# A four-stage transformer kernel on one core: x fetched per batch, a small constant tile, and late weight copies on ScalarE

## The chip, the cores and the metric

The kernel runs on one core of one Trainium2 chip. The metric is the device time of one execution in microseconds (us): the median of three runs of the kernel before. Lower is better.

## What is computed

The reference takes x of shape 32 x 256 x 128 (32 batches of 256 tokens, width 128) and sends it through four stages, each with a residual sum and a layer norm behind it:

```python
x = L0_attn_x
x = _layernorm(x + _L0_attn_ref(x, L0_attn_w_qkv, L0_attn_w_out, L0_attn_b_out), axis=-1)
x = _layernorm(x + _L0_ffn_ref(x, L0_ffn_W_fc, L0_ffn_ln_w, L0_ffn_ln_b, L0_ffn_W_proj), axis=-1)
x = _layernorm(x + _L1_attn_ref(x, L1_attn_ln_g, L1_attn_ln_b, L1_attn_W_kv, L1_attn_W_x, L1_attn_W_xa, L1_attn_W_out), axis=-1)
x = _layernorm(x + _L1_ffn_ref(x, L1_ffn_w_gate, L1_ffn_w_up, L1_ffn_w_down), axis=-1)
return x
```

The first attention has 16 heads of width 8 with rotary embedding. The first feed-forward rounds its weights to -1, 0 and 1 against their mean magnitude. The second attention mixes its heads by a 16 x 16 matrix. The second feed-forward scales integer weights by 1/127 and gates with silu.

## The kernel before

The program runs five sequences, one for each engine, that are written out by hand in `program`. Each phase (`early` and `late` of the preparation, `attn0`, `ffn0`, `attn1`, `ffn1`) gives each engine a step for one batch, and the engines meet only in semaphores. Software pipelining is explicit: in step i an engine works on batches i-2 to i+4. The first attention has 32 steps and some before and behind them; the middle ones run in a loop of two steps per turn, one for even and one for odd batches. Nothing reorders the instructions: each engine takes them as they are written.

**Preparation.** `early` loads the attention's weights (`raw_qkv`, `raw_out`), turns them on TensorE and copies them out of PSUM on VectorE (`w0_qk`, `w0_v`, `w0_out`); the copies set `attn_taken`, for which TensorE waits before it turns the first x. GpSimd fills `ident`, `zeros` and both `stack` buffers. SyncE waits for `stacks_set`, then writes the free slots of the DRAM scratch (`score_parts`) out of `stack`, and only then issues the first two loads of x (`x_in`, step -4 and -3). `late` prepares all other weights. On SyncE it issues the loads of `raw_fc`, `raw_proj`, `w1_kv`, `w1_out` and then four block loads of the whole x into `x_all`, before step -2. On ScalarE it issues nine loads, behind the first `x_t` copy. On VectorE it runs one chain: `cols`, `b0_out`, eight strided copies that make `mix`, `w1_qk`, the sums of the magnitudes, the rounding, the copies `w1_gate`, `w1_up`, `w1_down` and `w0_fc`, the products `scaled_proj` and `shift_cols`, `turned_proj`, and `w0_proj` and `c0_proj` at the end. On TensorE `late` stands between step -2 and step -1 and ends in a wait for `late_taken`, so TensorE can't begin the scores of batch 0 before it.

**A step of the first attention.** TensorE runs 16 slots s, one per head. In each it computes the second scores of batch i (`second_score`, L1053) and the first scores of batch i+1 (`first_score`, L1067). VectorE takes the maximum of the first scores (L918); ScalarE takes the exponential of the second scores (L865) into `probs`; the second scores of slot s wait until the exponential of slot s-2 has left its bank. Between them lie the products with the values (L1004), the projections q and k of batch i+3 (L1122, slots 4 and 6), the turned heads of batch i-1 (L1133, slot 8), their scaling on VectorE (`recips` L891, `o` L900) and the transposition of `o` (L1150, slot 10). GpSimd computes in each step, in this order: `x_v` (L705), `added` = `x_all` + bias for batch i-1 (`add_bias`, L655), the factors of the norm of batch i-2 (`norm_factor`, L691 to L698: `shifted_var`, `minus_mean`, `rstd`, `norm_shift`), and the split of q and k of batch i+3 into three bf16 parts (`split`, L744 to L760). ScalarE applies the norm of batch i-2 in slots 5 and 6 (L797), so it waits there for `norm_shift`.

**SyncE's step.** It loads `x_in` of batch i+4 (L627), moves the second half of the shift rows (L576), waits until the two stack loads of the step before have landed, writes the parts of batch i+2 to DRAM in ten DMAs (L596 to L599), waits until they have landed, and loads the stack of batch i+2 in two halves (L609). The first half waits for TensorE's slot 7, the second for slot 15.

## Time and profile before

| what | before |
|---|---|
| median of 3 runs | 1577.44 us (1575.67 to 1577.63) |
| the profiled execution's own time | 1577.22 us |
| its span, first to last instruction | 1574.7 us |
| TensorE busy | 1482.3 us (94%) |
| VectorE busy | 1205.6 us (77%) |
| ScalarE busy | 1045.4 us (66%) |
| GpSimd busy | 974.8 us (62%) |

The span is cut into 40 slices of 39 us in the profile; slices 1 to 13 are the first attention. TensorE's busy share is 0.3 in the first slice and 0.8 in the second, and 0.9 or more in the eleven after them. The DMA engines are busy 0.7 in the first slice and 0.4 in the rest of the first attention. The median and the profiled execution differ by 0.2 us, and 2.5 us of the profiled time lie outside the span.

### The profile page before, as it was taken

The page shows a single profiled execution, that of the slowest core. Times are in us where ns is not written, and L with a number is a line of the kernel's source. Part 1 is how long each engine was busy: PE and PEld are TensorE (multiplying, and loading weights), DVE is VectorE, ACT ScalarE, POOL GpSimd, SP SyncE. Part 2 cuts the span into 40 slices and gives each one's busy share as a digit, 9 for nine tenths or more (in the row PEclk, how much of TensorE's full clock was granted, in tenths as well). Part 3 has the DMA queues.
Part 4 walks back from the last instruction along what each step waited for, and adds up shares of the span by engine and source line. Part 5 has one row for each costly group of instructions (what it writes and reads, how often), then busy time and mean ns, then how long its engine had stood idle before and what let it go on. Part 6 is the DMA issues. An engine that isn't in the chain of part 4 may idle for free. (4 is left out here: it accounts for less than half of the span.)

```text
span 1574.7 us, 55380 instructions
## 1 busy us (share of the span) xinstructions
PE 1482.3 (94%) x17644; PEld 1136.0 (72%) x17644; DVE 1205.6 (77%) x3356; ACT 1045.4 (66%) x2564; POOL 974.8 (62%) x1161
## 2 busy tenths in 40 slices
PE   3899999999999899978999999999999999998998
PEld 2444444444444389967888889888888889897997
DVE  6787888888888568866778878787788878774666
ACT  0376777777777788855767777777777777774332
POOL 5355556565655157775787778777887778762222
PEclk8799999999999999987999999999999999999999
DMA  7444444444444200022222222222222222200121
GB/s 190 135 121 129 121 135 127 128 127 129 134 121 127 56 31 30 33 77 69 84 78 79 68 87 74 78 70 83 78 81 79 67 87 74 75 30 28 60 67 50
DMA packets 175163, 137.77 MB, mean 87 GB/s; under 512 B 13868, under 2 KB 144056, under 8 KB 175096
## 3 DMA queue, kind: packets, MB, share of 16 engines
q1 hardware_dynamic: 174128, 136.30, 30.1%
q8 instruction: 39, 0.64, 0.2%
q10 hardware_dynamic: 968, 0.60, 0.1%
q14 instruction: 28, 0.23, 0.0%
HBM read 68.95 MB, written 54.79 MB: 79 GB/s over the span
## 5 line engine op out<-in xcount | busy, mean ns | idle before, releaser
L918 DVE TENSOR_REDUCE shifts<-bank 128x2 bf16<-128x512 f32 x1024 | 690.5, 688 | 171.4 <-PE bank L1067 168.1
L865 ACT ACTIVATE probs<-bank 128x512 f32<-128x512 f32 x1024 | 577.0, 594 | 122.3 <-PE bank L1053 118.0
L1015 PE MATMUL bank<-values,probs 64*128 64x129 f32 x8192 | 579.8, 277 | 3.9 <-DVE o_even L885 0.7
L1015 PEld LDWEIGHTS bank<-values,probs 64*128 64x128 f32 x8192 | 526.9, 188 | 31.1 <-issue 11.0
L1053 PE MATMUL bank<-stack 49*128 49x256 bf16 x2048 | 366.2, 274 | 9.4 <-DMA stack<-shift_rows 6.1
L1067 PE MATMUL bank<-stack 48*128 48x256 bf16 x2048 | 364.6, 276 | 10.7 <-DVE shifts L918 5.8
L666 POOL TENSOR_TENSOR values<-mix,v_in 128x1024 f32<-128x1024 f32 x128 | 302.1, 2361 | 0.0
L675 POOL TENSOR_TENSOR o_odd<-o_odd,scaled 128x256 f32<-128x256 f32 x224 | 163.5, 730 | 162.5 <-ACT scaled L789 162.2
L1053 PEld LDWEIGHTS bank<-stack 49*128 49x128 bf16 x2048 | 165.7, 95 | 94.8 <-ACT probs L865 35.7
L789 ACT ACTIVATE scaled<-bank,recips 128x128 f32<-128x128 f32 x448 | 138.0, 358 | 88.5 <-DVE recips L912 88.5
L1067 PEld LDWEIGHTS bank<-stack 48*128 48x128 bf16 x2048 | 157.4, 96 | 34.3 <-DVE shifts L918 18.4
L1004 PE MATMUL bank<-probs,values 128*32 128x256 f32 x2048 | 164.7, 394 | 0.0
L744 POOL TENSOR_TENSOR exact<-turned 128x512 f32<-128x512 f32 x32 | 40.7, 1273 | 176.4 <-DVE turned L940 163.7
L885 DVE SCALAR_TENSOR_TENSOR o_even<-bank,recips,o_even 128x128 f32<-128x128 f32 x448 | 136.7, 347 | 8.1 <-DVE recips L912 0.3
L912 DVE RECIPROCAL recips<-bank 128x2 f32<-128x2 f32 x512 | 84.6, 165 | 62.5 <-PE bank L1015 53.2
L1004 PEld LDWEIGHTS bank<-probs,values 128*32 128x32 f32 x2048 | 40.6, 108 | 54.3 <-issue 51.4
L1122 PE MATMUL bank<-x_t,w_qk 128*128 128x256 f32 x256 | 78.2, 433 | 0.9 <-ACT x_t L852 0.9
L771 ACT ACTIVATE shift_rows<-bank 8x256 bf16<-8x256 bf16 x128 | 46.8, 365 | 44.4 <-PE bank L986 44.2
L1469 PE MATMUL bank<-w_proj,h_t_f 128*128 128x129 f32 x512 | 71.7, 284 | 4.0 <-DVE square_sums_f L1435 4.0
L1469 PEld LDWEIGHTS bank<-w_proj,h_t_f 128*128 128x128 f32 x512 | 64.8, 195 | 7.6 <-issue 5.8
L1122 PEld LDWEIGHTS bank<-x_t,w_qk 128*128 128x128 f32 x256 | 47.3, 205 | 31.3 <-issue 24.9
L1562 POOL TENSOR_TENSOR var_f<-moments_f,ln_shift 128x2 f32<-128x2 f32 x32 | 6.3, 197 | 102.3 <-DVE moments_f L1620 102.3
(169 smaller groups left out, 2158.8 us busy)
## 6 DMA issues: line engine op xcount, KB each, us to landing
stack<-score_parts SPq DMA_DIRECT2D x64, 512.0 KB, 3.9
stack<-score_parts SPq DMA_DIRECT2D x256, 96.0 KB
score_parts<-parts SPq DMA_DIRECT2D x256, 64.0 KB, 2.1
score_parts<-parts SPq DMA_DIRECT2D x128, 96.0 KB, 2.3
score_parts<-parts SPq DMA_DIRECT2D x64, 192.0 KB, 2.3
x_in_f<-x_all SPq DMA_DIRECT2D x64, 128.0 KB, 2.0
score_parts<-parts SPq DMA_DIRECT2D x64, 128.0 KB, 2.3
x_in<-in_L_attn_x SPq DMA_DIRECT2D x32, 128.0 KB, 3.6
```

The source lines that it names most:

```text
L666: pool.tensor_tensor(values[i.plus(1).odd][:, t, heads, 0:D], core.mix[:, heads, :], v_in[:, t, :].unsqueeze(1).broadcast_to([P, half_head ...
L675: pool.tensor_tensor(o_odd[b.odd][:, :, :], o_odd[b.odd][:, :, :], scaled[:, h // 2 % 4, :, :], op=ALU.add).then_inc(odd_added, 1)
L789: act.activation(to, pv_bank(h)[:, t * (D + 1):t * (D + 1) + D], ACT.Copy, scale=recips[:, h % 2, t:t + 1]).then_inc(scaled_ready, 1)
L865: act.activation(probs[:, s % RING, :, :].rearrange("p t n -> p (t n)"), s2[s % 2][:, :], ACT.Exp, scale=scale).then_inc(exp_done, 1)
L885: dve.scalar_tensor_tensor(o_even[b.odd][:, t, :], part, recips[:, h % 2, t:t + 1], o_even[b.odd][:, t, :], op0=ALU.mult, op1=ALU.add).the ...
L918: dve.tensor_reduce(shifts[:, :, hf, col], s1_bank(s)[:, :].rearrange("p (t n) -> p t n", t=TILES), op=ALU.max, axis=AX.X, negate=True).th ...
L1004: last = pe.matmul(pv[0][VW * a:VW * (a + 1), 0:TOK], values[b.odd][:, t, :, :].rearrange("p h c -> p (h c)")[:, start:start + VW], probs[ ...
L1015: return pe.matmul(pv_bank(h)[:, q * (D + 1):(q + 1) * (D + 1)], probs[rows, h % RING, t, q * P:(q + 1) * P], values[b.odd][rows, t, h, :] ...
L1053: score = pe.matmul(s2[s % 2][:, t * TOK:(t + 1) * TOK], core.k_stack[b.odd][rows, s // 2, t * P:(t + 1) * P], core.q_stack[b.odd][rows, s ...
L1067: score = pe.matmul(s1_bank(s)[:, t * TOK:(t + 1) * TOK], core.q_stack[b.odd][rows, h // 2, t * P:(t + 1) * P], core.k_stack[b.odd][rows, ...
L1122: last = pe.matmul((m1, m0)[side][:, v * TOK:(v + 1) * TOK], core.w0_qk[:, side, v, :], x_t[b.odd][:, :], start=True, stop=True)
L1469: pe.matmul(out_banks[i.odd][:, t * width:t * width + D + 1], h_t[i.odd][:, c, own], core.w0_proj[:, c, :], start=(c == 0), stop=(c == chu ...
```

## The change

SyncE's order changes: the two first `x_in` loads now stand ahead of the four writes of the free slots, and the four block loads of x are gone. The free slots are filled out of `free_rows`, a tile of 128 x 256 bf16, and the fills of both stacks are gone with `stacks_set`. `x_all` of batch i is now loaded at the end of SyncE's step i (steps 0 to 31), and `add_bias` waits for that batch alone. The nine weight loads of ScalarE move from `late` to `early`. `mix`, `b0_out`, `w1_gate`, `w1_up`, `w1_down`, `w0_fc` and `turned_proj` are copied by ScalarE.

```diff
     def _(sp):
         sp.dma_start(raw_qkv[:, :, :], w["w_qkv"].rearrange("(t e) d -> e t d", e=D)).then_inc(load_attn, 16)
         sp.dma_start(raw_out[:, :], w["w_out0"]).then_inc(load_attn, 16)
         sp.dma_start(core.rope[:, :, :], w["rope"]).then_inc(load_rope, 16)
-        sp.wait_ge(stacks_set, 3)
+
+    @late.engine("sync")
+    def _(sp):
+        sp.wait_ge(free_rows_set, 1)
         for side in range(2):
             for parity in range(2):
-                sp.dma_start(scratch[side, parity, USED:SLOTS, :, :].rearrange("s (d r) n -> (s d) (r n)", r=PAIRS),
-                             core.stack[0][0:(SLOTS - USED) * HD, side, :, :].rearrange("p r n -> p (r n)")
-                             ).then_inc(free_slots_written, 16)
-
-    @late.engine("sync")
-    def _(sp):
+                sp.dma_start(scratch[side, parity, USED:SLOTS, :, :].rearrange("s q n -> (s q) n"),
+                             free_rows[:, :]).then_inc(free_slots_written, 16)
...
-        for k in range(core.x_all_loads):
-            sp.dma_start(to[:, k * tiles:(k + 1) * tiles, :], x[:, k * tiles:(k + 1) * tiles, :]).then_inc(core.x_all_loaded, 16)
...
+    @late.engine("scalar")
+    def _(act):
+        act.wait_ge(cols_ready, 1)
+        mixed = bank[1][:, 128:384].rearrange("p (g h) -> p h g", h=HEADS)
+        for d in range(HD):
+            act.activation(core.mix[:, :, :].rearrange("p h (g d) -> p h g d", d=HD)[:, :, :, d], mixed, ACT.Copy)
+        act.activation(core.b0_out[:, :], bank[1][:, 384:512], ACT.Copy).then_inc(small_taken, 1)
+        act.wait_ge(ffn1_turned, 1)
+        for k, to in enumerate((core.w1_gate, core.w1_up, core.w1_down)):
+            act.activation(to[:, :, :].rearrange("p c d -> p (c d)"), bank[(4, 5, 0)[k]][:, 0:3 * D],
+                           ACT.Copy).then_inc(ffn1_taken, 1)
+        act.wait_ge(ffn0_turned, 1)
+        act.activation(core.w0_fc[:, :, :].rearrange("p c d -> p (c d)"), bank[2][:, :], ACT.Copy).then_inc(fc_taken, 1)
+        act.wait_ge(ffn0_turned, 2)
+        act.wait_ge(proj_scaled, 8)
+        act.activation(turned_proj[:, :, :].rearrange("p c d -> p (c d)"), bank[3][:, :], ACT.Copy).then_inc(proj_taken, 1)
...
-            pool.memset(stack[:, :, :, :].rearrange("p e r n -> p (e r n)"), 1.0).then_inc(stacks_set, 1)
+        pool.memset(free_rows[:, :], 1.0).then_inc(free_rows_set, 1)
...
-        pe.wait_ge(proj_scaled, 9)
+        pe.wait_ge(cols_ready, 1)
+        pe.wait_ge(small_taken, 1)
+        pe.wait_ge(proj_scaled, 8)
         for c in range(4):
             pe.matmul(bank[1][:, 0:D], ones[:, :], scaled_proj[:, c, :], start=(c == 0), stop=(c == 3))
+        pe.wait_ge(proj_taken, 1)
...
                 stack_in(i.plus(2), i, on, 1)
+            if first and on(0):
+                wait_apart(sp, core.x_all_loaded, times(i, -1, n) * 16)
+                sp.dma_start(core.x_all[:, i.number(), :, :], source[i.number(), :, :, :]).then_inc(core.x_all_loaded, 16)
...
         def add_bias(i):
-            pool.wait_ge(core.x_all_loaded, 16 * core.x_all_loads)
+            pool.wait_ge(core.x_all_loaded, times(i, -1, n) * 16)
...
-    final("tensor", late, late_taken=1)
+    final("tensor", late, late_taken=1, ffn1_taken=3, fc_taken=1)
```

SyncE at the program's start, before. `x_in_0` stands for either of the two input buffers, `score_parts` is the DRAM scratch:

```order
L261 DMA rope<-rope_tables 128x512
L265 DMA score_parts<-stack 16x2048 [waits stacks_set_early]
L265 DMA score_parts<-stack 16x2048 x3
L627 DMA x_in_0<-in_L_attn_x 128x2x128 x2
L271 DMA raw_fc<-in_L_ffn_W_fc 128x4x128
L272 DMA raw_proj<-in_L_ffn_W_proj 128x512
L273 DMA w_kv<-in_L_attn_W_kv 128x256
L274 DMA w_out<-in_L_attn_W_out 128x128
L280 DMA x_all<-in_L_attn_x 128x16x128 x4
L627 DMA x_in_0<-in_L_attn_x 128x2x128 [waits xt_in_psum_attn0,free_slots_written_early]
```

In the change:

```order
L266 DMA rope<-rope_tables 128x512
L631 DMA x_in_0<-in_L_attn_x 128x2x128 x2
L273 DMA score_parts<-free_rows 128x256 [waits free_rows_set_early]
L273 DMA score_parts<-free_rows 128x256 x3
L275 DMA raw_fc<-in_L_ffn_W_fc 128x4x128
L276 DMA raw_proj<-in_L_ffn_W_proj 128x512
L277 DMA w_kv<-in_L_attn_W_kv 128x256
L278 DMA w_out<-in_L_attn_W_out 128x128
L631 DMA x_in_0<-in_L_attn_x 128x2x128 [waits xt_in_psum_attn0,free_slots_written_early]
```

The first two loads of x moved ahead of the four writes of the free slots, and nothing stands any more between the weights' loads and the third load of x.

SyncE in the loop of the first attention, at the end of the even step and the start of the odd one, before:

```order
L609 DMA stack<-score_parts 128x2x1024 [waits s_in_psum_attn0]
L90 REGISTER_ALU
L627 ISA [waits xt_in_psum_attn0]
L627 DMA x_in_0<-in_L_attn_x 128x2x128
L90 REGISTER_ALU
L576 DMA stack<-shift_rows_0 2x4x256 [waits shift_rows_ready_attn0]
```

In the change:

```order
L613 DMA stack<-score_parts 128x2x1024 [waits s_in_psum_attn0]
L652 ISA [waits x_all_loaded]
L652 DMA x_all<-in_L_attn_x 128x2x128
L90 REGISTER_ALU
L631 ISA [waits xt_in_psum_attn0]
L631 DMA x_in_0<-in_L_attn_x 128x2x128
```

The load of `x_all` now stands where `x_in` stood, right behind the second half of the stack, and `x_in` follows it.

VectorE's chain in `late`, before, up to the products for the projection:

```order
L341 COPY cols<-bank 128x10 [waits load_rest_late,small_turned_late]
L342 COPY b_out<-bank 128x128
L345 COPY mix<-bank 128x256 x8
L346 COPY w_qk<-w_kv 128x128
L351 TENSOR_REDUCE totals<-raw_fc 128x1 [waits load_ffn0_late]
```

In the change:

```order
L351 COPY cols<-bank 128x10 [waits load_rest_late,small_turned_late]
L352 COPY w_qk<-w_kv 128x128
L357 TENSOR_REDUCE totals<-raw_fc 128x1 [waits load_ffn0_late]
L357 TENSOR_REDUCE totals<-raw_proj 128x1
L360 TENSOR_SCALAR scaled<-raw_int 128x1152 [waits load_ffn1_late]
```

Nine copies left VectorE between `cols` and `w1_qk`; five more left it further down (`w_gate`, `w_up`, `w_down`, `w_fc`, `turned_proj`).

## Rows read from the trace of the kernel before

**Rows 1.** Timeline of the start: start us, us, engine, line, operation.

```profile
1.69 6.97 POOL L307 MEMSET stack<- 128x4096 bf16 x2
...
5.70 3.04 DVE L333 COPY w_v<-bank 128x128 f32<-128x128 f32 x1
...
10.45 0.96 SPq L627 DMA_DIRECT2D x_in<-in_L_attn_x  x2
...
13.15 0.66 PE L1166 MATMUL bank<-ident,x_in 128*128 128x128 f32 x2 [8.42 <-DMA x_in<-in_L_attn_x]
```

**Rows 2.** Timeline, the way of batch 0 to its stack.

```profile
13.64 13.44 SPq L280 DMA_DIRECT2D x_all<-in_L_attn_x  x4
...
24.22 1.16 POOL L760 TENSOR_TENSOR parts<-rest,parts 128x512 bf16<-128x512 f32 x1
...
27.18 3.47 SPq L627 DMA_DIRECT2D x_in<-in_L_attn_x  x1
...
38.79 0.90 SPq L609 DMA_DIRECT2D stack<-score_parts  x2
...
44.19 0.59 SPq L596 DMA_DIRECT2D score_parts<-parts  x1
```

**Rows 3.** Timeline, VectorE's chain of the late weights.

```profile
24.44 0.28 DVE L342 COPY b_out<-bank 128x128 f32<-128x128 f32 x1
...
28.32 0.45 DVE L346 COPY w_qk<-w_kv 128x128 f32<-128x128 f32 x1
...
39.27 0.68 DVE L384 COPY turned_proj<-bank 128x512 f32<-128x512 f32 x1
...
44.26 0.28 DVE L391 COPY c_proj<-bank 128x128 f32<-128x128 f32 x1
```

**Rows 4.** Timeline of one step of the loop, from the stack's first half to slot 10.

```profile
318.52 0.37 SPq L609 DMA_DIRECT2D stack<-score_parts  x1
...
321.73 0.37 SPq L609 DMA_DIRECT2D stack<-score_parts  x1
...
322.45 0.39 SPq L627 DMA_DIRECT2D x_in<-in_L_attn_x  x1
...
322.52 0.28 PE L1067 MATMUL bank<-stack 48*128 48x256 bf16 x1
...
322.76 0.73 POOL L655 TENSOR_TENSOR added<-x_all,b_out 128x256 f32<-128x256 f32 x1 [0.37 <-DVE y L949]
...
324.33 0.20 POOL L691 TENSOR_TENSOR shifted_var<-moments,ln_shift 128x2 f32<-128x2 f32 x1 [0.84 <-DVE moments L964]
...
325.48 0.20 POOL L698 TENSOR_TENSOR norm_shift<-minus_mean,rstd 128x2 f32<-128x2 f32 x1
...
327.40 0.48 ACT L797 ACTIVATE x_all<-y,norm_shift,rstd 128x128 f32 x1
...
327.78 0.59 ACT L865 ACTIVATE probs<-bank 128x512 f32<-128x512 f32 x1
...
328.88 0.27 PE L1053 MATMUL bank<-stack 49*128 49x256 bf16 x1
...
330.48 0.38 PE L1067 MATMUL bank<-stack 48*128 48x256 bf16 x2
...
331.18 0.64 DVE L918 TENSOR_REDUCE shifts<-bank 128x2 bf16<-128x512 f32 x1
...
332.25 0.44 PE L1150 MATMUL bank<-ident,o 128*128 128x128 f32 x2 [0.72 <-DVE o L900]
```

**Rows 5.** Last line of the view of L609 (stack loads), 250 to 480 us.

```profile
DMA to landing us min/median/max: 3.7/4.0/4.2
```

**Rows 6.** The same line of the view of L627 (loads of `x_in`).

```profile
DMA to landing us min/median/max: 3.2/3.6/3.9
```

**Rows 7.** Waits from 128 to 145 us: in total, times, longest.

```profile
PE bank L1067 <- DMA stack<-score_parts: 0.7, 1, 0.7
```

**Rows 8.** One stretch: busy PE, PEld, DVE, ACT, POOL, granted clock, DMA share, GB/s.

```profile
139.00:140.00 1.00, 1.00 (x9) 0.20 (x2) 0.87 (x2) 0.70 (x3) 0.20 (x1) 0.50 0.02 4
```

More of the change, by code:

```diff
@@ L233, in prepare @@
     ident_step = early.sem("ident_step")
-    stacks_set = early.sem("stacks_set")
+    free_rows_set = early.sem("free_rows_set")
+    zeros_set = early.sem("zeros_set")
     free_slots_written = early.sem("free_slots_written")
@@ L255, in prepare @@
     late_taken = late.sem("late_taken")
+    small_taken = late.sem("small_taken")
+    ffn1_taken = late.sem("ffn1_taken")
+    fc_taken = late.sem("fc_taken")
+    proj_taken = late.sem("proj_taken")
     @early.engine("sync")
@@ L274, in _ @@
         sp.dma_start(core.w1_out[:, :], w["w_out1"]).then_inc(load_rest, 16)
-        x = w["x"].rearrange("b (t p) d -> p (b t) d", p=P)
-        to = core.x_all[:, :, :, :].rearrange("p b t d -> p (b t) d")
-        tiles = core.n * TILES // core.x_all_loads
-        for k in range(core.x_all_loads):
-            sp.dma_start(to[:, k * tiles:(k + 1) * tiles, :], x[:, k * tiles:(k + 1) * tiles, :]).then_inc(core.x_all_loaded, 16)
     @early.engine("scalar")
-    def _(act):
-        pass
-    @late.engine("scalar")
     def _(act):
@@ L303, in _ @@
                            base=0, pattern=[[-1, P]], channel_multiplier=1).then_inc(ident_step, 1)
-        pool.memset(core.zeros[:, :], 0.0).then_inc(stacks_set, 1)
-        for stack in core.stack:
-            pool.memset(stack[:, :, :, :].rearrange("p e r n -> p (e r n)"), 1.0).then_inc(stacks_set, 1)
-        pool.wait_ge(stacks_set, 3)
+        pool.memset(free_rows[:, :], 1.0).then_inc(free_rows_set, 1)
+        pool.memset(core.zeros[:, :], 0.0).then_inc(zeros_set, 1)
+        pool.wait_ge(zeros_set, 1)
     @late.engine("gpsimd")
@@ L341, in _ @@
         dve.tensor_copy(core.cols[:, :], bank[1][:, 0:10]).then_inc(cols_ready, 1)
-        dve.tensor_copy(core.b0_out[:, :], bank[1][:, 384:512])
-        mixed = bank[1][:, 128:384].rearrange("p (g h) -> p h g", h=HEADS)
-        for d in range(HD):
-            dve.tensor_copy(core.mix[:, :, :].rearrange("p h (g d) -> p h g d", d=HD)[:, :, :, d], mixed)
         dve.tensor_copy(core.w1_qk[:, :].rearrange("p (a d r) -> p a d r", a=2, d=HD),
@@ L383, in _ @@
                               ALU.mult).then_inc(proj_scaled, 1)
-        dve.tensor_copy(turned_proj[:, :, :].rearrange("p c d -> p (c d)"), bank[3][:, :]).then_inc(proj_scaled, 1)
         dve.memset(core.w0_proj[:, :, D:D + 1], 1.0)
@@ L1680, in program @@
     attn0.at(-4, -3)
[L1681 removed]
+    if kind == "sync":
         late.begin(kind, eng)
```

9 lines of the change are left out of this document (2 added, 7 removed).

## The prediction

> **What bounds the kernel now.** I read the timeline of the start first, since the whole change is in the preparation and in the first attention; then the timeline of one step of the first attention's loop; then the views of the lines that load the stack and x; last the waits around the one place in that stage where TensorE waits for a DMA. In the start the reader is to look for what TensorE waits for. It turns the first x at 13.15 after 8.42 us of waiting for the load of x, which SyncE issued only at 10.45, behind the free slots' writes and so behind GpSimd's fill of the stacks, 1.69 to 8.66 [rows 1]. From there two chains run side by side and meet again at the first scores of batch 0. One is the stack of batch 0: GpSimd has the parts ready at 25.38 (24.22 + 1.16), but SyncE is held in the block loads of x (13.64 + 13.44) and in the x load behind them until 30.65; the stack is asked for at 38.79, and at 44.19 SyncE goes on, having waited for it to land [rows 2]. The other is VectorE's chain of late weights, which ends at 44.54 (44.26 + 0.28) [rows 3]. So both must become shorter, and both do. In the loop the reader is to see how little room there is: the row of GpSimd's `added`, the norm's first row on ScalarE, and TensorE's wait of 0.72 for `o` [rows 4].
>
> **Start.** The fill of the stacks (two fills, 6.97 us) becomes one of a sixteenth of one stack, so SyncE's first x loads go out right behind `rope`, at about 2.2. Landing takes 3.2 to 3.9 us [rows 6], so x is there at 5.4 to 6.1. Now TensorE's other wait decides, `attn_taken`. VectorE starts the copy `w0_v` at 5.70, and its record is drawn out to 8.74, just behind the end of GpSimd's fill [rows 1]; the same form of copy, `b0_out`, takes 0.28 [rows 3]. Without the hold, `w0_v` and `w0_out` end at 5.70 + 2 x 0.28 = 6.26. The first transposition then starts at about 6.3 and not 13.15: **6.85 us** are gained. Bounds: if the hold had another cause than the fill, `w0_v` still ends at 8.74, `w0_out` 0.3 later, and the gain is 4.1 (13.15 - 9.05); it can't be above 7.1, since x lands at 6.1 or so. I take 6.85, since the drawn-out records and the fill end together.
>
> The nine loads on ScalarE now start at about 0.8 and run beside `raw_qkv` and x. Their table load and nine issues are over before the first `x_t` copy is due at about 7.0, so the price is their traffic alone. The row of this case: x's load takes 3.6 us beside a stack load, so I add nothing. A page speaks against this step: the Trainium skill, "DMA: Bandwidth & Descriptors", section "Issuing engines are not separate DMA queues", says that DMAs issued from different engines run on the same 16 DMA engines and interleave, so that a second issuer saves only issue time. By it the weight loads (0.58 MB) would delay x by the time of their bytes; my estimate is up to 2 us, which would make the sum 1.5 us worse. No row of before shows the two together.
>
> **Stack of batch 0.** Its parts are ready 6.85 us earlier, at 18.5, and SyncE is free by then: behind x it issues four writes and four loads, eight issues of half a microsecond, done near 7. From 30.65 the ten writes, their landing and the stack took until 44.19, 13.5 us [rows 2]. So it lands at 18.5 + 13.5 = **32.1**, 12.1 us earlier.
>
> **Late weights.** VectorE loses `b0_out` and the eight copies of `mix`: from 24.44 to 28.32 = 3.88 us [rows 3]. `w_gate`, `w_up` and `w_down` were copied while TensorE still turned `raw_proj`, so their removal is worth nothing. `w_fc` has the form of `turned_proj` and cost VectorE its 0.6 right behind that; `turned_proj` itself, started at 39.27 for 0.68 [rows 3], stood between the last product and TensorE's sums, another 0.6. Sum: 6.85 + 3.88 + 0.6 + 0.6 = 11.9, so the chain ends at 44.54 - 11.9 = **32.6**. What ScalarE takes over is hidden: by the exponential's row a copy of 128x512 takes at most 0.6 [rows 4], eight of half that size end near 21, and they are wanted only by TensorE's sums near 28; `turned_proj` now waits for all eight products and takes 0.6 while TensorE does the first sums. If that cover failed, its 0.6 would come back. The later of the two chains decides: batch 0's scores start **11.9 us** earlier, and everything behind them moves along. Bounds 8 and 13.5.
>
> **The loop.** The load of `x_all` for batch i-1 is issued right behind the second half of the stack, where `x_in` stood: 0.65 us behind it, at 322.4. Against the issue of the stack at S = 321.73, `x_in` was issued at S + 0.7 and lands after 3.2 to 3.9 [rows 4, 6], the stack itself at S + 4.0 [rows 5]. I put `x_all` in its place, with data behind the stack's: landed at S + 4.4, bounds S + 3.9 and S + 5.1 (if it shares with `x_in`, issued 0.6 later, and lands with it at the longest time). `added` begins some 0.25 us later, at S + 4.65; before it began at S + 1.03 [rows 4]. What it had for cover: the four steps of the norm factor follow, which waited 0.84 us for `moments`, and from `shifted_var` to the end of `norm_shift` it is 325.68 - 324.33 = 1.35 [rows 4]. Now they start as soon as `added` ends: `norm_shift` ends at S + 4.65 + 0.7 + 1.35 = S + 6.7. ScalarE wants it at 327.40 = S + 5.67 [rows 4]. So ScalarE waits some 1.05 us in slot 5, with the exponentials of slots 5 on queued behind it. In the other step of the loop S stands 0.2 us earlier against the norm, and the wait is 0.85.
>
> Who waits for that: the exponential of slot 5 ended at 328.37 and TensorE's second score of slot 7, which needs its bank, began at 328.88 [rows 4], so 0.5 us are covered and TensorE slips 0.35 to 0.55. VectorE wants the first scores of slot 8, whose last matmul ends at about 330.75, only at 331.18 [rows 4]: another 0.4 are covered, for TensorE waits 0.72 us for `o` at slot 10 anyway. What is left per step is 0 to 0.3 us; I take 0.17. The norm and a late `x_all` meet in steps 2 to 30, 29 steps: **+5 us**. At the bounds of the landing it is 0 and about 0.8 x 29 = 23 us.
>
> There is a second limit that the same load touches. The first half of the stack, issued at 318.52 and landing after 4.0, is there at 322.5, and TensorE's first score that needs it begins at 322.52 [rows 4, 5]: that path has no slack. It hangs on the stack's second half through SyncE's wait before the ten writes. If `x_all` slows that landing by 0.1 to 0.2, the path is longer by as much, but it runs beside the slip above and is covered by it, so I add nothing.
>
> **Sum.** 1577.2 (the profiled execution, 0.2 below the median) - 11.9 + 5 = 1570.3; I say **1570**.
>
> **Rivals.** A, the load lands early enough (by S + 4.2) or the slip vanishes in TensorE's wait for `o`: 1577.2 - 11.9 = 1565. For it: 0.72 us of that wait; against: the load can hardly pass the stack in front of it. B, the other side: `x_all` and `x_in` share the queue and `x_all` lands near S + 5.0. ScalarE then waits 1.5 us, and 0.6 per step is left, 17 us: 1577.2 - 11.9 + 17 = 1582, slower. The point from which it decides is a slip of 0.41 us a step (11.9 / 29), that is a landing at about S + 4.75. A page would have it so: the Trainium skill, "DMA: Bandwidth & Descriptors", section "Two DMAs through the same engine are not ordered", says that descriptors in a queue start in order but are pipelined. In this mechanism also belongs that a longer wait drops TensorE's clock: between 128 and 145 us it once waited 0.7 for a stack, and the granted clock from 139 to 140 is 0.50, the level of 1.2 GHz [rows 7, 8]. C, the preparation gives only part (x or the parts come later than I say, about 5 us less): 1575, hardly to be told from no change. D, that the change doesn't reach the end, since a later stage waits for something else: nothing of the later stages depends on absolute time, so I give it nothing.
>
> **Chances.** My forecast 0.45, A 0.2, B 0.17, C 0.18. A difference under 0.2% (3.2 us) is about what a measurement of this kernel can't tell from none. The forecast and A lie below 1574.2, C on the edge, B above 1580.6 for the most part: faster 0.68, within 0.2% 0.18, slower 0.14. The range leaves out the worst of B and a little of A: 1564 to 1581.
>
> **What will show it.** In the start: the first transposition of x at 6 to 7 us, the stack's landing near 32, VectorE's chain ending near 32.6, the first L1067 near 33. In the loop: `added` released by the DMA of `x_all` and no more by `y`; `norm_shift` ending behind S + 6.5; an idle time of about 1 us before L797 on ScalarE, ended by GpSimd; the wait of L1150 for `o` shorter than 0.72; steps longer by 0.1 to 0.2 us. It would be wrong if ScalarE doesn't wait there (A), if L1150 still waits 0.7 while the steps are longer by half a microsecond or the clock is at 0.5 in the loop (B), or if the first transposition comes after 8 us (C).

## The result, and the profile after

The changed kernel takes **1586.43 us** (median of 16 runs, 1579.5 to 1593.71), the kernel before beside it 1578.03 us (16 runs, 1575.56 to 1582.38): ratio **1.0054**, 95% interval 1.0042 to 1.0066. It is slower by about 8.5 us where 1570 was forecast. The profiled execution took 1589.78 us, its span is 1588.0 us.

Four marks divide the span. The first scores of batch 0 start at 37.15 us and not at 44.97, 7.8 earlier. From there to the first transposition of `o` it is 38.7 us (37.9 before). The marks of the loop are the first and the last of its 32 transpositions of `o`. Timeline of the changed kernel (start us, us, engine, line, operation, idle before and its releaser):

```profile
75.85 0.44 PE L1157 MATMUL bank<-ident,o 128*128 128x128 f32 x2 [0.72 <-DVE o L907]
...
568.84 0.44 PE L1157 MATMUL bank<-ident,o 128*128 128x128 f32 x2 [0.97 <-DVE o L907]
```

and the same two in the kernel before:

```profile
82.89 0.44 PE L1150 MATMUL bank<-ident,o 128*128 128x128 f32 x2 [0.72 <-DVE o L900]
...
555.16 0.44 PE L1150 MATMUL bank<-ident,o 128*128 128x128 f32 x2 [0.97 <-DVE o L900]
```

So the loop went from 472.3 to 493.0 us, +20.7, where +5 was forecast. What follows lasts 1019 us in both. The sum: -7.8 + 0.8 + 20.7 - 0.4 = +13.3, the difference of the two spans (1588.0 - 1574.7). That is more than the 8.5 of the medians: the profiled execution is 3.4 us above the median of its kernel. The start gave less than forecast, and the loop took four times as much. Of the 20.7, 22 steps from the middle of the loop (steps 5 to 26), the mean of which went from 15.38 to 15.99 us, say what each step costs: **+0.61 us**. The rest, 7.2 us, lies in the first four steps (+0.6) and in the last five (+6.6), which vary from run to run.

**The loop, one step.** These rows answer to [rows 4]; lines of the code after the load stand 4 to 7 further down than before (L613 is the stack's load, L652 the new load, L662 `added`, L705 `norm_shift`, L804 the norm, L872 the exponential, L1060 and L1074 the scores, L925 the shifts, L1157 the transposition of `o`).

```profile
322.49 0.38 SPq L613 DMA_DIRECT2D stack<-score_parts  x1
...
323.14 0.41 SPq L652 DMA_DIRECT2D x_all<-in_L_attn_x  x1
...
327.12 0.72 POOL L662 TENSOR_TENSOR added<-x_all,b_out 128x256 f32<-128x256 f32 x1 [4.68 <-DMA x_all<-in_L_attn_x]
...
328.95 0.20 POOL L705 TENSOR_TENSOR norm_shift<-minus_mean,rstd 128x2 f32<-128x2 f32 x1
...
329.33 0.49 ACT L804 ACTIVATE x_all<-y,norm_shift,rstd 128x128 f32 x1 [1.07 <-POOL norm_shift L705]
...
330.36 0.28 PE L1060 MATMUL bank<-stack 49*128 49x256 bf16 x1 [0.56 <-ACT probs L872]
...
332.02 0.36 DVE L898 RECIPROCAL recips<-bank 128x32 f32<-128x32 f32 x1 [0.26 <-PE bank L1140]
...
333.52 0.44 PE L1157 MATMUL bank<-ident,o 128*128 128x128 f32 x2 [0.42 <-DVE o L907]
```

With S = 322.49: `added` starts at S + 4.63, and no more at S + 1.03 [rows 4], and GpSimd stood idle for 4.68 us before it. `norm_shift` ends at S + 6.66, the norm starts at S + 6.84 after 1.07 us of waiting. TensorE then waits for the exponential that is queued behind it, VectorE waits at L898 for the heads that TensorE turns (L1140), and the transposition of `o` starts at S + 11.03, where it was S + 10.52 (332.25 - 321.73 [rows 4]): 0.51 later. The same over the loop, waits from 100 to 500 us (in total, times, longest):

```profile
POOL added L662 <- DMA x_all<-in_L_attn_x: 119.3, 25, 5.2
...
ACT x_all L804 <- POOL norm_shift L705: 30.4, 25, 1.4
...
PE bank L1060 <- ACT probs L872: 17.6, 25, 0.9
PE bank L1157 <- DVE o L907: 10.5, 25, 0.4
PE bank L1074 <- DVE shifts L925: 4.3, 26, 0.4
```

In the kernel before the same view of TensorE has neither a wait of L1053 for the exponentials nor more than 1.3 us for the shifts:

```profile
PE bank L1150 <- DVE o L900: 18.0, 25, 0.7
PE bank L1067 <- DVE shifts L918: 1.3, 8, 0.2
```

Per step of TensorE: +17.6/25 = 0.70 for the exponential, +3.0/25 = 0.12 for the shifts, -7.5/25 = 0.30 at `o`: 0.52 of the 0.61.

Where the slip passes through VectorE, its timeline in the kernel before (330 to 332.3 us) has no idle time:

```profile
330.32 0.69 DVE L918 TENSOR_REDUCE shifts<-bank 128x2 bf16<-128x512 f32 x1
330.92 0.35 DVE L891 RECIPROCAL recips<-bank 128x32 f32<-128x32 f32 x1
...
331.73 0.47 DVE L900 TENSOR_TENSOR o<-bank,recips 128x128 f32<-128x128 f32 x2
```

and in the changed kernel (331 to 333.5 us):

```profile
331.07 0.69 DVE L925 TENSOR_REDUCE shifts<-bank 128x2 bf16<-128x512 f32 x1
...
332.98 0.48 DVE L907 TENSOR_TENSOR o<-bank,recips 128x128 f32<-128x128 f32 x2
```

The first of these rows still stands at S + 8.6 in both. The turned heads of TensorE, which the reciprocal reads, in the kernel before and in the changed one:

```profile
329.76 0.66 PE L1133 MATMUL bank<-ident,heads_t 128*128 128x128 f32 x4
```

```profile
331.33 0.66 PE L1140 MATMUL bank<-ident,heads_t 128*128 128x128 f32 x4
```

They were ready at S + 8.69, half a microsecond before VectorE took them, and are ready at S + 9.50 now. The reciprocal starts at S + 9.53 and not at S + 9.19, 0.34 later, and `o` at S + 10.49 and not at S + 10.00, 0.49 later.

**The start.** Timeline of the changed kernel, the rows that answer to [rows 1 to 3]:

```profile
6.89 0.66 PE L1173 MATMUL bank<-ident,x_in 128*128 128x128 f32 x2 [1.55 <-DVE w_out L344]
...
19.52 3.92 ACT L297 ACTIVATE mix<-bank 128x256 f32<-128x256 f32 x8 [5.75 <-DVE cols L351]
...
25.76 1.63 DVE L377 SCALAR_TENSOR_TENSOR raw_fc<-raw_fc,bounds,below 128x512 f32<-128x512 f32 x1
27.32 1.21 DVE L377 SCALAR_TENSOR_TENSOR raw_proj<-raw_proj,bounds,below 128x512 f32<-128x512 f32 x1
...
31.74 0.60 ACT L307 ACTIVATE turned_proj<-bank 128x512 f32<-128x512 f32 x1 [2.54 <-DVE shift_cols L384]
31.79 2.05 PE L431 MATMUL bank<-scaled_proj,ones 128*128 128x128 f32 x8 [2.09 <-DVE shift_cols L384]
...
32.49 0.59 SPq L600 DMA_DIRECT2D score_parts<-parts  x1
...
36.19 0.28 DVE L392 COPY c_proj<-bank 128x128 f32<-128x128 f32 x1
```

The fill no longer holds `w_v`, whose copy takes 0.28 us, and TensorE turns x at 6.89 (forecast 6.3). SyncE goes on at 32.49, behind the stack (forecast 32.1). ScalarE's copies are hidden, as argued. But VectorE's chain ends at 36.47 and not at 32.6. Two of its rows stand out: the second half of the rounding, 1.63 and 1.21 us, took 0.74 and 0.74 in the kernel before.

### The profile page after: what moved, and what is told of

It reads as the page before. It is cut to its first block and busy times, and to the rows that moved or that the text cites. A ratio compares the mean times of both kernels' runs of the same rounds, so it can differ in the third digit from the quotient of the medians.

```text
span 1588.0 us, 55503 instructions
## 1 busy us (share of the span) xinstructions
PE 1491.7 (94%) x17644; PEld 1136.7 (72%) x17644; DVE 1202.1 (76%) x3342; ACT 1052.2 (66%) x2578; POOL 966.5 (61%) x1160
## 5 line engine op out<-in xcount | busy, mean ns | idle before, releaser
L925 DVE TENSOR_REDUCE shifts<-bank 128x2 bf16<-128x512 f32 x1024 | 691.8, 690 | 175.9 <-PE bank L1074 173.1
L872 ACT ACTIVATE probs<-bank 128x512 f32<-128x512 f32 x1024 | 576.1, 593 | 113.7 <-PE bank L1060 109.6
L1060 PE MATMUL bank<-stack 49*128 49x256 bf16 x2048 | 369.7, 275 | 30.1 <-ACT probs L872 25.8
L1074 PE MATMUL bank<-stack 48*128 48x256 bf16 x2048 | 371.8, 278 | 12.5 <-DVE shifts L925 8.8
L1060 PEld LDWEIGHTS bank<-stack 49*128 49x128 bf16 x2048 | 164.2, 95 | 122.4 <-ACT probs L872 54.8
L1074 PEld LDWEIGHTS bank<-stack 48*128 48x128 bf16 x2048 | 155.8, 96 | 35.8 <-DVE shifts L925 22.2
L662 POOL TENSOR_TENSOR added<-x_all,b_out 128x256 f32<-128x256 f32 x32 | 23.2, 725 | 173.7 <-DMA x_all<-in_L_attn_x 153.1
L804 ACT ACTIVATE x_all<-y,norm_shift,rstd 128x128 f32 (+1 forms) x128 | 59.1, 492 | 40.8 <-POOL norm_shift L705 40.8
L778 ACT ACTIVATE shift_rows<-bank 8x256 bf16<-8x256 bf16 x128 | 46.8, 365 | 38.7 <-PE bank L993 38.4
```

The costliest lines, as they stand in the source:

```text
L872: act.activation(probs[:, s % RING, :, :].rearrange("p t n -> p (t n)"), s2[s % 2][:, :], ACT.Exp, scale=scale).then_inc(exp_done, 1)
L925: dve.tensor_reduce(shifts[:, :, hf, col], s1_bank(s)[:, :].rearrange("p (t n) -> p t n", t=TILES), op=ALU.max, axis=AX.X, negate=True).th ...
L1060: score = pe.matmul(s2[s % 2][:, t * TOK:(t + 1) * TOK], core.k_stack[b.odd][rows, s // 2, t * P:(t + 1) * P], core.q_stack[b.odd][rows, s ...
L1074: score = pe.matmul(s1_bank(s)[:, t * TOK:(t + 1) * TOK], core.q_stack[b.odd][rows, h // 2, t * P:(t + 1) * P], core.k_stack[b.odd][rows, ...
```

## The experiments

**My theory (W)**: the loop loses by GpSimd's wait for `x_all`, which makes `norm_shift` late, then ScalarE, then TensorE. **Rival (T)**: the traffic of 128 KB more in the stack's queue costs it, wherever one waits for it. All ratios are against the kernel before on the same chip, with 95% intervals; what a profile shows is one execution of each kernel. The first four shared 17 runs of the kernel before (median 1576.66 us).

**e1_ahead.** The load of `x_all`, in the same place of the queue, for the batch that is needed a step later:

```diff
-            if first and on(0):
-                wait_apart(sp, core.x_all_loaded, times(i, -1, n) * 16)
-                sp.dma_start(core.x_all[:, i.number(), :, :], source[i.number(), :, :, :]).then_inc(core.x_all_loaded, 16)
+            if first and on(1):
+                b = i.plus(1)
+                wait_apart(sp, core.x_all_loaded, times(i, 0, n) * 16)
+                sp.dma_start(core.x_all[:, b.number(), :, :], source[b.number(), :, :, :]).then_inc(core.x_all_loaded, 16)
```

> The changed kernel with one edit: at the end of SyncE's step i it loads x_all of batch i+1, not of batch i. The issue stands at the same place with the same bytes, but GpSimd's wait is for data that landed a step ago. Theory W (the loop loses by GpSimd's wait for the load, which delays norm_shift and so ScalarE in slot 5): added starts at S + 1.0 again (S is the issue of the second half of the stack), ScalarE's idle time before the norm is gone, the steps go from 16.0 back to 15.4 us, and the time falls by about 17 us, to 1570. Theory T (the loop loses by the traffic of the extra 128 KB a step, which lands the stacks later): the steps stay near 16.0 and the time stays at 1586.

Measured: 1569.05 us, ratio **0.9953** (0.9938 to 0.9968), steps 15.48 us. Timeline of this kernel, the same step:

```profile
329.30 0.38 SPq L613 DMA_DIRECT2D stack<-score_parts  x1
...
329.96 0.40 SPq L653 DMA_DIRECT2D x_all<-in_L_attn_x  x1
...
330.30 0.72 POOL L663 TENSOR_TENSOR added<-x_all,b_out 128x256 f32<-128x256 f32 x1 [0.33 <-DVE y L957]
...
331.90 0.19 POOL L699 TENSOR_TENSOR shifted_var<-moments,ln_shift 128x2 f32<-128x2 f32 x1 [0.88 <-DVE moments L972]
...
334.96 0.48 ACT L805 ACTIVATE x_all<-y,norm_shift,rstd 128x128 f32 x1
...
339.82 0.44 PE L1158 MATMUL bank<-ident,o 128*128 128x128 f32 x2 [0.72 <-DVE o L908]
```

The load is issued at S + 0.66, as in the changed kernel, and its traffic is there. `added` waits for `y` again, the norm for nothing, and TensorE 0.72 us for `o`: every row stands as in [rows 4].

**e2_norm_first.** The load stays late, but the norm factor goes ahead of the adding on GpSimd:

```diff
-            if on(-1):
-                add_bias(i)
             if on(-2):
                 norm_factor(i)
+            if on(-1):
+                add_bias(i)
```

> The changed kernel with GpSimd's norm_factor ahead of add_bias in its step; the load of x_all stays where it is and as late as it is. Theory W: norm_shift ends near S + 4.1, ScalarE doesn't wait, steps of 15.4, time near 1570, as with the load a step ahead. Theory T: 16.0 and 1586. If this one recovers less than the load a step ahead, the late add delays something behind it on GpSimd (the split of q and k).

Measured: 1566.03 us, ratio **0.9927** (0.9911 to 0.9944), steps 15.49 us. ScalarE doesn't wait for the norm, though the load lands as late as before and GpSimd still waits for it. Timeline of this kernel:

```profile
336.99 0.19 POOL L705 TENSOR_TENSOR norm_shift<-minus_mean,rstd 128x2 f32<-128x2 f32 x1
...
337.87 0.72 POOL L662 TENSOR_TENSOR added<-x_all,b_out 128x256 f32<-128x256 f32 x1 [0.69 <-DMA x_all<-in_L_attn_x]
```

**e3_mid.** The load of `x_all` one place earlier in the queue, ahead of the second half of the stack:

```diff
-            if on(2):
-                stack_in(i.plus(2), i, on, 1)
             if first and on(0):
                 wait_apart(sp, core.x_all_loaded, times(i, -1, n) * 16)
                 sp.dma_start(core.x_all[:, i.number(), :, :], ...).then_inc(core.x_all_loaded, 16)
+            if on(2):
+                stack_in(i.plus(2), i, on, 1)
```

> The changed kernel with the load of x_all of batch i issued just before the second half of the stack, where SyncE waits for TensorE's slot 15 anyway. Theory W: it lands some 1 to 2 us behind S or earlier, GpSimd isn't held, steps of 15.4, time 1570. If the traffic right behind the stack's second half matters too (the stack landed at S + 4.2 in the changed kernel against S + 4.0 before), this one is a little faster than the load a step ahead, by 0.1 us a step or 3 us in all.

Measured: 1570.17 us, ratio **0.9963** (0.9949 to 0.9976), steps 15.55 us. Waits of GpSimd from 100 to 500 us in this kernel:

```profile
POOL added L662 <- DMA x_all<-in_L_attn_x: 30.4, 25, 4.2
```

GpSimd still waits, 1.2 us a time in the mean, and ScalarE hardly ever does: a wait of this length is covered. The step of 15.4 that I expected didn't come, nor the 0.1 us a step that this place was to gain on e1_ahead.

**e4_loop_only.** The kernel before with nothing but the load moved into the loop (its preparation as before, without the four block loads):

```diff
-        for k in range(core.x_all_loads):
-            sp.dma_start(to[:, k * tiles:(k + 1) * tiles, :], x[:, k * tiles:(k + 1) * tiles, :]).then_inc(core.x_all_loaded, 16)
...
+            if first and on(0):
+                wait_apart(sp, core.x_all_loaded, times(i, -1, n) * 16)
+                sp.dma_start(core.x_all[:, i.number(), :, :], source[i.number(), :, :, :]).then_inc(core.x_all_loaded, 16)
...
-            pool.wait_ge(core.x_all_loaded, 16 * core.x_all_loads)
+            pool.wait_ge(core.x_all_loaded, times(i, -1, n) * 16)
```

> The kernel before with the load of x alone changed: no block loads, x_all of batch i at the end of SyncE's step i, and add_bias waiting for it. The rest of the preparation is as before. My reading: the stack of batch 0 lands 5 us earlier, but VectorE's late chain still ends at 44.5 or a little before, so the start gains at most 1 us, and the loop costs 0.6 x 28 = 17 us: about 1594. If the time is near 1586 the block loads alone were worth as much as the whole preparation's change.

Measured: 1593.09 us, ratio **1.0112** (1.0091 to 1.0134), steps 15.99 us, VectorE's late chain ends at 44.81, before at 44.54. So the load alone costs 0.0112 x 1577 = 17.7 us. Waits from 100 to 500 us in this kernel, beside those of the changed one:

```profile
POOL added L651 <- DMA x_all<-in_L_attn_x: 118.4, 25, 5.2
...
PE bank L1049 <- ACT probs L861: 17.1, 25, 1.0
```

W holds, and T falls for all but a small part: where nobody that matters waits for the load, a step is 0.1 to 0.2 us longer than before (15.45 to 15.58 in the profiles of the repaired kernels, against 15.38) and not 0.61.

**e12_behind** raises the dose (it shared 11 runs of the kernel before, median 1578.62). The changed kernel, with the load of `x_all` one place later in the queue, behind `x_in`:

```diff
                 sp.dma_start(x_in[b.odd][:, :, :], src).then_inc(x_loaded[b.odd], 16)
+            if first and on(-1):
+                b = i.plus(-1)
+                wait_apart(sp, core.x_all_loaded, times(i, -2, n) * 16)
+                sp.dma_start(core.x_all[:, b.number(), :, :], source[b.number(), :, :, :]).then_inc(core.x_all_loaded, 16)
...
-            if first and on(0):
-                wait_apart(sp, core.x_all_loaded, times(i, -1, n) * 16)
-                sp.dma_start(core.x_all[:, i.number(), :, :], source[i.number(), :, :, :]).then_inc(core.x_all_loaded, 16)
```

> The changed kernel, but x_all of the batch behind is loaded after x_in instead of ahead of it: the dose of the suspected wait is raised. x_all is issued about 0.75 us later and should land at S + 5.1 to S + 5.5 instead of S + 4.5. If GpSimd's wait sets the slip, nothing covers the rest: norm_shift ends 0.6 to 0.8 us later, ScalarE waits 1.8 to 2 us instead of 1.17, and a step of the loop is longer by 0.6 to 0.8 us again: about 16.7 instead of 15.99, the time 18 to 22 us above the changed kernel's (ratio about 1.018). Rival: the slip in the loop comes from the traffic of the load and not from the wait for it; then moving it changes next to nothing, the ratio stays near 1.0054.

Measured: 1590.26 us, ratio 1.0073 (1.0053 to 1.0093), steps 16.26 us. The dose came out smaller than I wanted: `x_all` lands at S + 4.85 in the mean and at S + 4.56 in the changed kernel, 0.29 later and not 0.6 to 1.0. The answer is as large as the dose. Waits from 100 to 500 us in this kernel:

```profile
PE bank L1061 <- ACT probs L873: 25.0, 25, 1.3
PE bank L1158 <- DVE o L908: 10.5, 25, 0.4
```

TensorE waits 1.00 us and not 0.70 for the exponential, +0.30; the wait for `o` stays at 0.42; a step costs +0.27, so hardly anything of the additional wait is covered. By time alone the two kernels can't be told apart (their intervals overlap); by their loops they can: steps of 15.99 us and 493.0 us in all in the changed kernel, 16.26 and 497.2 here.

**The start, term by term.** These kernels undo one part each, on e1_ahead as their base. e9_ahead_again is that base once more, beside the same 11 runs of the kernel before as e10 to e12.

> The kernel of e1_ahead once more, to have the base of the single edits measured beside the kernel before with more runs. Expected: the same as e1_ahead within its interval, a ratio of 0.995 (0.9938 to 0.9968). In the preparation its late chain should again end between 33 and 36, as in e1_ahead, e2_norm_first and e3_mid, whose preparation is the same.

Measured: 1570.41 us, ratio 0.9938 (0.9916 to 0.996). Its late chain ends at 33.55, in e1_ahead at 33.82.

**e5_copies_back** gives all copies back to VectorE, at their old places. There are 14 (`b0_out`, eight of `mix`, three of the second feed-forward's weights, `w0_fc` and `turned_proj`); the expectation's thirteen is a miscount. Shown are the first nine:

```diff
+        dve.tensor_copy(core.b0_out[:, :], bank[1][:, 384:512])
+        mixed = bank[1][:, 128:384].rearrange("p (g h) -> p h g", h=HEADS)
+        for d in range(HD):
+            dve.tensor_copy(core.mix[:, :, :].rearrange("p h (g d) -> p h g d", d=HD)[:, :, :, d], mixed)
```

> The change with x_all loaded a step ahead, and the thirteen copies of late weights given back to VectorE (ScalarE only loads). This measures one term of the prediction's sum by itself, against e1_ahead (1569.05 us). The prediction's sum: VectorE's late chain ends 3.88 + 0.6 + 0.6 = 5.1 us later, at about 38.9 instead of 33.8, and the time is 1569.05 + 5.1 = 1574. Rival: the chain is not what sets the first scores (the stack's landing at about 32 is near it, and TensorE's products at its lower clock can set the pace of the chain by themselves), so that less than half comes back: 1570 to 1571.

Measured: 1572.93 us, ratio 0.9963 (0.9947 to 0.998); 23 runs of the kernel before shared by e5 to e8, median 1578.45. The late chain ends at 37.52, 3.8 us behind the base (33.55 to 33.82), where the sum had 5.1. Of the 1.3 us that are missing, 0.9 is the rounding: it comes later here and lies less beside GpSimd's split, and its four rows take 4.82 us and not 5.70 (see e7_split_later). By time it is 1.6 to 3.9 us slower than the base (5.1 expected).

**e6_start_back** puts the fill of both stacks and the free slots' writes ahead of x again:

```diff
+        sp.wait_ge(zeros_set, 3)
+        for side in range(2):
+            for parity in range(2):
+                sp.dma_start(scratch[side, parity, USED:SLOTS, :, :].rearrange("s (d r) n -> (s d) (r n)", r=PAIRS),
...
+        for stack in core.stack:
+            pool.memset(stack[:, :, :, :].rearrange("p e r n -> p (e r n)"), 1.0).then_inc(zeros_set, 1)
```

> The change with x_all loaded a step ahead, but the fill of both stacks and the writes of the free slots stand ahead of the first x load again, as before the change. This measures the first term of the sum, against e1_ahead (1569.05 us). The prediction's sum: the first transposition of x goes from about 6.9 back to about 13.15, and 6.25 to 6.85 us come back: 1569.05 + 6.5 = 1575.5. Rival: after the later start TensorE and VectorE go through the preparation faster (VectorE's rounding took 1.63 us with GpSimd's split beside it, and 0.74 before the change, and TensorE's lower clock falls on other work), so that the first scores come back by only 3 to 4 us: 1572.5.

Measured: 1576.37 us, ratio 0.9979 (0.9964 to 0.9994). Timeline of this kernel:

```profile
13.14 0.66 PE L1176 MATMUL bank<-ident,x_in 128*128 128x128 f32 x2 [8.41 <-DMA x_in<-in_L_attn_x]
...
40.10 0.28 DVE L394 COPY c_proj<-bank 128x128 f32<-128x128 f32 x1
```

The first transposition is back at 13.14, and the late chain ends at 40.38, 6.7 us later than in the base: the term of 6.85 is there whole. By time it is 4.1 to 6.5 us slower than the base (6.5 expected).

**e7_split_later** holds GpSimd before the split of batch 1 until VectorE has rounded:

```diff
     attn0.at(-4, -3)
+    final("gpsimd", late, ternary_ready=2)
```

> The change with x_all loaded a step ahead, and GpSimd held before the split of batch 1 until VectorE has rounded the late weights. It tests whether GpSimd's work beside VectorE is what lengthens the rounding (1.63 and 1.21 us against 0.74 and 0.74 before the change). If so, these rows are 0.74 again and the late chain ends some 1.5 to 2 us earlier than in e1_ahead (about 32 instead of 33.8); the time is up to 2 us below 1569.05, less if the parts of batch 1 then come too late for its stack in the first step. Rival: the durations have another cause (TensorE's banks, the loads), the rows stay above 1.2 and nothing is won; then holding GpSimd can only cost, up to 3 us.

Measured: 1565.76 us, ratio **0.992** (0.9894 to 0.9946). The four rows of the rounding in its base, e1_ahead:

```profile
19.49 0.84 DVE L372 TENSOR_SCALAR below<-raw_fc,bounds 128x512 f32<-128x512 f32 x1
20.26 1.48 DVE L372 TENSOR_SCALAR below<-raw_proj,bounds 128x512 f32<-128x512 f32 x1
21.66 1.74 DVE L377 SCALAR_TENSOR_TENSOR raw_fc<-raw_fc,bounds,below 128x512 f32<-128x512 f32 x1
23.33 1.64 DVE L377 SCALAR_TENSOR_TENSOR raw_proj<-raw_proj,bounds,below 128x512 f32<-128x512 f32 x1
```

and in e7_split_later, where GpSimd waits until they are done:

```profile
19.31 0.49 DVE L372 TENSOR_SCALAR below<-raw_fc,bounds 128x512 f32<-128x512 f32 x1
19.71 0.48 DVE L372 TENSOR_SCALAR below<-raw_proj,bounds 128x512 f32<-128x512 f32 x1
20.11 0.74 DVE L377 SCALAR_TENSOR_TENSOR raw_fc<-raw_fc,bounds,below 128x512 f32<-128x512 f32 x1
20.77 0.74 DVE L377 SCALAR_TENSOR_TENSOR raw_proj<-raw_proj,bounds,below 128x512 f32<-128x512 f32 x1
```

The four rows are 5.70 us together in the base and 2.45 here. Of the 3.2 us gained, 1.2 to 1.5 reach the end of the chain (32.35), since the split now runs beside the next rows of VectorE: three of its four `shift_cols` take 1.05 to 1.16 us here, against 0.27 to 0.96 in the base. So the cause of the long rows is shown by the rows; by time the kernel can't be told from its base, as the intervals overlap.

**e10_loads_later** puts ScalarE's nine weight loads back behind the first `x_t` copy, where they stood before the change (they become a stage of their own that begins there; nothing else differs). The expectation says "its first two"; in the trace they are issued from 6.83 on, between the first copy and the second (12.15).

> The change with x_all loaded a step ahead, and ScalarE's nine weight loads back behind its first two x_t copies. The prediction gave weight loads first no gain and no cost. The page's rule that I set beside it (the loads run on the same 16 DMA engines as x and would delay it by up to 2 us) says that the first transposition of x comes earlier without them than the 6.2 to 6.9 us of the runs so far, down to about 5.5, and all up to 1.5 us earlier. The other side: the weights of the late chain land later, by some 8 us, and if VectorE has to wait for them the late chain ends later than 33 to 36. I expect the first transposition at 6.2 to 6.4 and a time within 2 us of e9_ahead_again.

Measured: 1569.43 us, ratio 0.9941 (0.992 to 0.9962), against 0.9938 of its base. The first transposition comes at 6.13, in the base at 6.39; the late chain ends at 33.21 and 33.55. The traffic does reach x: its first two loads land at 5.33 and 5.70, in the base at 5.97 and 7.05 (5.35 to 6.67 and 6.54 to 7.43 in all kernels with the weight loads first and x ahead). But in both kernels the first transposition waits for the copy of `w_out` and not for x (in e1_ahead it was x, at 6.80), and the second x isn't wanted before 11. So most of it is covered, and by time the order of these loads gives nothing and takes nothing that can be measured.

**e8_both** and **e11_norm_split** look for a better kernel: e1_ahead and e2_norm_first together, and e2_norm_first and e7_split_later together.

> Both repairs together: x_all loaded a step ahead, and the norm factor ahead of the adding of the bias on GpSimd. If each of them takes the whole of the slip in the loop away, they don't add up: 1566 to 1569, as either alone, ScalarE's idle time ahead of the norm 0, TensorE's wait for o 0.72. Rival: e2_norm_first (1566.03) was faster than e1_ahead (1569.05) by something of its own (the factor is ready earlier, in the tail too), which adds to what loading ahead gives: then below 1565.

> The version that the runs so far point to: the change with GpSimd's norm factor ahead of the adding of the bias (as e2_norm_first) and GpSimd held before the split of batch 1 until VectorE has rounded the late weights (as e7_split_later). If the two gains are separate, ScalarE's idle time before the norm is 0, TensorE waits 0.72 us for o, the rounding takes 0.5 and 0.74 us a row, the late chain ends at 32 to 32.5, and the time is at or below the better of the two (0.992 of before, 1565.8). Rival: the held split makes the stack of batch 1 late in the first step, and with the x_all load in that step it shows: first step above 18.2, and a ratio of 0.995 or more.

Measured: e8_both 1567.98 us, ratio 0.992 (0.9893 to 0.9947); e11_norm_split 1567.65 us, ratio 0.9927 (0.9904 to 0.9951). The repairs of the loop don't add up, as either takes the slip away. e11's late chain ended at 34.66 and not at 32 to 32.5, as expected: its rounding is as short as in e7_split_later (2.44 us), but began 2.3 us later (21.61 and 19.31), by the uneven start that the last section describes. e2, e7, e8 and e11, at 0.992 to 0.9927, can't be told from one another. Each beats both the kernel before (by about 12 us) and the changed one (by about 20); whether e2 is better than e1_ahead itself the intervals leave open. The smallest edit of them is e2_norm_first: two calls exchanged.

## Why the prediction was wrong

**The step that failed** is the size of what is left per step of the loop: "What is left per step is 0 to 0.3 us; I take 0.17". It is 0.61 (e4_loop_only: 17.7 us in all), so the term of 5 us was 17.7. The chain of causes was right at each link down to VectorE, and most of its sizes:

- `x_all` landed at S + 4.56 in the mean (forecast 4.4, bounds 3.9 to 5.1), and in the step shown `added` began at S + 4.63 (4.65) and `norm_shift` ended at S + 6.66 (6.7). Right.
- ScalarE's wait: 30.4/25 = 1.22 (forecast 1.05 and 0.85, so 0.95). Short by 0.27: the norm starts 0.18 behind the end of `norm_shift`, which I had put at 0, and over the 25 steps `norm_shift` ends at S + 6.82 in the mean, 0.12 later than forecast.
- TensorE's slip at slot 7: 0.70 (0.35 to 0.55). The cover of 0.5 by the exponential was right (1.22 - 0.70), so the 0.27 comes through whole.
- VectorE's cover of 0.4: there is one of 0.5, but at the reciprocal and not at the scores of slot 8. In the step shown the turned heads come 0.81 later (0.72 at slot 7 and 0.09 on the way), and the reciprocal 0.34. But 0.15 is lost again in the two rows behind it. In the kernel before, the reciprocal and the shifts behind it each started before the row ahead had ended (0.81 us from the reciprocal's start to that of `o`); in the changed kernel, where the reciprocal had to wait, it takes 0.96.
- TensorE's wait of 0.72 for `o`: I named it as what swallows the rest, and it swallows nothing. `o` itself hangs on VectorE, whose rows in front of it left no idle time in the kernel before, so `o` comes as late as VectorE does, and the shorter wait (0.42) says only that TensorE, too, came later. This was the error of reasoning, beside the sizes: an engine that waits at a place is no cover if what it waits for slips as well.
- So 0.34 + 0.15 = 0.49 of the 0.61 is the wait. About 0.1 is not: the steps of e1_ahead (15.48) and e2_norm_first (15.49), where ScalarE doesn't wait, are still longer than the 15.38 of before. I had given the additional traffic nothing. The second half of the stack lands 4.18 us after its issue in e1_ahead, and 4.02 in the kernel before, in the means of 26; that this causes the 0.1 wasn't tried. In e3_mid, where `x_all` goes ahead of this half, it lands after 4.31 and the steps are 15.55.
- The prediction's own terms give 0.95 - 0.5 - 0.4 = 0.05 a step; I took 0.17. With the measured wait they give 0.32. So about half of what was missing is the wait, and half is the loss behind the reciprocal and the part that isn't the wait at all.

**The start** gave 8 to 11 us, not 11.9; I take 10.5, the middle of the seven profiles with the same preparation. The late chain ends at 33.2 to 33.8 in four (e1_ahead, e3_mid, e9_ahead_again, e12_behind), and at 35.72, 35.88 and 36.47 in e2_norm_first, e8_both and the changed kernel; before it was 44.54. The two groups differ in TensorE's pace at the beginning (last section), and the one profile of the kernel before has the slow pace: like with like the gain is about 8 to 9. By time the changed kernel is 9 us faster than e4_loop_only (give or take 4), which differs from it in the preparation alone. The first term (6.85) was right: e6_start_back 6.7. The terms of the copies (5.1 in all) were 3.8: e5_copies_back. What I left out, beside the pace: moving VectorE's rounding earlier put it beside GpSimd's split of batch 1. The four rows took 3.80 us in the kernel before (1.38, 0.94, 0.74, 0.74), 5.70 in e1_ahead and 2.45 alone. The Trainium skill, "SBUF — State Buffer", section "Who interferes with whom", says that a VectorE instruction with two inputs in SBUF contends with a GpSimd instruction that reads SBUF. L377 has two such inputs, the split reads SBUF, and the trace agrees: 0.74 us without the split, 1.64 to 1.74 beside it. It says the same of tensor_scalar in one of its modes, and L372 goes from 0.48 to 1.48; in which mode L372 ran no row says. I held what VectorE gains against VectorE's own rows and didn't look at who would be its neighbour.

**The sum by measured terms**: -10.5 + 17.7 = +7.2 (+7 to +10 with the start's whole range), against +8.5 measured. In the prediction's own words the result is rival B's side, its point of decision a slip of 0.41 us a step; that point was right, and the slip passed it. But B's mechanism is not what happened: `x_all` landed at S + 4.56, short of the S + 4.75 that B wanted. I had tied the slower outcome to the landing alone, and it came from a wait and a cover that I had sized wrongly at the landing I expected. The section of the Trainium skill that was B's witness ("DMA: Bandwidth & Descriptors", "Two DMAs through the same engine are not ordered") speaks of loads that start in order and are pipelined. Here `x_all`, issued 0.65 us behind the stack, landed about 0.36 behind it (4.56 and 4.20 in the means), and in e12_behind, issued 1.4 or 1.9 behind it, at S + 4.85: 0.97 later at the issue was 0.29 later at the landing.

**The other page** that I weighed, the rule of the 16 DMA engines in the Trainium skill, "DMA: Bandwidth & Descriptors", section "Issuing engines are not separate DMA queues", would by the prediction's estimate have made the start up to 1.5 us worse. The trace agrees on the direction: without the weight loads beside it x lands 0.6 us earlier, and the second x 1.3 (e10_loads_later). Of this 0.3 us at most reach the first transposition, which waits for another load.

**The clock** was not the cause. From 100 to 500 us, where the steps are longer, the changed kernel shows no fall of the granted clock, and its mean over the span is 0.979, 0.975 in the kernel before. It has a part in the last steps, in that one execution: near the end of the stage 13.6 us are at 0.50, 3.4 in the kernel before, and 10 us at half the clock are worth up to 5 of the 6.6 us by which the last five steps are longer (my estimate). This is one such stretch (busy PE, PEld, DVE, ACT, POOL, granted clock, DMA share, GB/s):

```profile
521.50:531.50 10.00, 10.00 (x68) 4.25 (x72) 4.74 (x10) 5.24 (x12) 0.00 (x0) 0.50 0.35 94
```

0.50 is the level of 1.2 GHz. One or two such stretches stand near the end of this stage in every kernel, 3 to 17 us long, and with them come last steps that differ by some us.

## What to carry to other kernels

When a load is moved next to its use, look at what stands behind the waiting instruction in its engine's queue: here a 0.7 us addition that nobody needed for a step stood ahead of a 1.35 us chain that ScalarE needed at once. Exchange the two, or load a step ahead, and the wait costs nothing (what is left, 0.1 us a step, is not the wait). An idle time that an engine shows further on covers a slip only if what it waits for there isn't late by the same slip: follow the slip through the releasers, not along one engine.

## What the runs showed of the hardware that I had not expected

- GpSimd beside VectorE lengthens single rows of VectorE by about 1 us: a 128x512 f32 scalar_tensor_tensor from 0.74 to 1.74, a 128x512 tensor_scalar from 0.48 to 1.48, a 128x128 tensor_scalar from 0.27 to 1.16 (e1_ahead and e7_split_later). Which rows are long moves with the split.
- TensorE's first rows differ from run to run. The eight products of the second batch take, in the changed kernel and in e1_ahead (timelines of each):

```profile
13.81 3.78 PE L1129 MATMUL bank<-x_t,w_qk 128*128 128x256 f32 x8 [0.47 <-ACT x_t L859]
```

```profile
13.21 1.99 PE L1130 MATMUL bank<-x_t,w_qk 128*128 128x256 f32 x8 [0.47 <-ACT x_t L860]
```

The seven profiles with the same preparation fall into two groups by this row: 1.99 or 2.00 us and a late chain that ends at 33.2 to 33.8, or 3.20 to 3.78 us and 35.7 to 36.5. The 2 to 3 us between them are more than most of the terms above; what decides between the two wasn't tried.
